# Sixty unread products of ones in the tail of a fused cross-attention, differential attention and expert-mixture kernel

## The reference, cut to what matters

```
x = x + cross_attention(ctx_1024, layernorm(x))      # 16 batches, 64 queries, 1601 + 64 keys, 16 heads of 64
x = x + differential_attention(layernorm(x))         # 16 heads, pairs of 8 columns, causal, group norm, Wo
x = x + experts(layernorm(x))                        # 8 experts, gates are a softmax over the two largest logits
# experts:
logits = x @ gate_w.T + gate_b ; keep the top 2, softmax
expert_out = einsum('bsd,edo->bseo', x, expert_w) + expert_b
out = einsum('bseo,bse->bso', expert_out, gate_score)
```

## Time and profile before

| what | us |
|---|---|
| median of 3 runs | 997.82 |
| lowest and highest of them | 996.78, 1000.93 |
| time of the profiled execution | 998.82 |
| its span | 997.1 |
| of that, what lies around the span | 1.72 |
| TensorE busy | 944.7 |
| mean granted clock of TensorE | 0.974 of full speed |

### The profile page before, as it was taken

How to read it: one execution, slowest core, us unless ns; L and a number is a source line. 1 busy time by engine, 2 the same in 40 slices (tenths; PEclk the granted TensorE clock), 3 DMA queues, 4 the chain that set the end, 5 groups by cost and what they waited for, 6 DMA issues and landing times.

```text
span 997.1 us, 19671 instructions
## 1 busy us (share of the span) xinstructions
PE 944.7 (95%) x7942; PEld 501.6 (50%) x7942; DVE 782.8 (79%) x1540; ACT 738.6 (74%) x1017; POOL 376.0 (38%) x376
## 2 busy tenths in 40 slices
PE   8679999999999999999999999999999998969975
PEld 5434455454545454545454545454545454547742
DVE  5968796969696969696969696969695956658965
ACT  4576878787878787878787878787878776635631
POOL 6471143433333343434343434343434223143343
PEclk9799999999999999999999999999999999979987
DMA  6212020302020312121212121121212000000000
GB/s 204 68 22 58 11 79 15 76 17 74 18 73 18 73 17 73 23 68 25 66 24 67 23 68 33 59 37 54 32 48 35 22 2 22 1 23 23 2 7 16
DMA packets 73218, 41.79 MB, mean 42 GB/s; under 512 B 60932, under 2 KB 68520, under 8 KB 73128
## 3 DMA queue, kind: packets, MB, share of 16 engines
q1 hardware_dynamic: 72840, 39.49, 16.4%
q10 hardware_dynamic: 288, 1.05, 0.3%
HBM read 25.98 MB, written 0.59 MB: 27 GB/s over the span
## 4 chain that ended last, share of the span: by engine, by line
PE 81%; DVE 13%; ACT 2%; issue 2%; POOL 1%; DMA 1%; POOLq 0%; ACTq 0%; DVEq 0%
PE S L1977 10%; PE S L1985 9%; PE S L1979 9%; PE OA L2006 9%; PE OA L2008 9%; PE OA L2010 9%; PE WW L1942 8%; PE WW L1958 1%; PE WW L1960 1%; DVE mx L1417 1%; PE WW L1959 1%; PE WW L1929 1%; DVE amx L720 1%; PE WW L1931 1%; PE WW L1930 1%
## 5 line engine op out<-in xcount | busy, mean ns | idle before, releaser
L1429 DVE TENSOR_TENSOR region<-S,region 128x1024 f16<-128x1024 f32 (+1 forms) x224 | 272.1, 1215 | 107.5 <-ACT S L1726 106.8
L1721 ACT ACTIVATE region<-S,sigma 128x1024 f16<-128x1024 f32 (+1 forms) x224 | 250.3, 1117 | 121.4 <-PE S L1985 121.4
L1417 DVE TENSOR_REDUCE mx<-WW 128x1 f32<-128x512 f32 (+1 forms) x480 | 263.6, 585 | 29.9 <-PE WW L1942 21.2
L1726 ACT ACTIVATE S<-S,sigma 128x1024 f32<-128x1024 f32 (+1 forms) x224 | 244.1, 1090 | 0.0
L1977 PE MATMUL S<-region,xT_hi 128*128 128x512 f16 (+1 forms) x416 | 124.3, 380 | 3.4 <-DVE region L1429 2.2
L2006 PE MATMUL OA<-region,xk 128*128 128x512 f16 (+1 forms) x416 | 124.4, 381 | 0.0
L1985 PE MATMUL S<-region,xT_lo 128*128 128x512 f16 (+1 forms) x416 | 124.2, 380 | 0.0
L2008 PE MATMUL OA<-region,xk 128*128 128x512 f16 (+1 forms) x416 | 124.2, 380 | 0.0
L1979 PE MATMUL S<-region,xT_hi 128*128 128x512 f16 (+1 forms) x416 | 124.1, 380 | 0.0
L2010 PE MATMUL OA<-region,xk 128*128 128x512 f16 (+1 forms) x416 | 124.0, 380 | 0.0
L1942 PE MATMUL WW<-xT_hi,region 128*128 128x512 f16 x360 | 120.3, 380 | 1.6 <-DVE region L1408 0.9
(11 more groups left out here) (296 smaller groups left out, 1728.3 us busy)
## 6 DMA issues: line engine op xcount, KB each, us to landing
raw<-ctx SPq DMA_DIRECT2D x16, 768.0 KB
rb<-inv_dram SPq DMA_DIRECT2D x16, 512.0 KB, 3.6
raw<-ctx SPq DMA_DIRECT2D x16, 32.5 KB
WO_lo<-L_xattn_Wq ACTq DMA_DIRECT2D x1, 512.0 KB, 3.9
WO_hi<-L_xattn_Wkv ACTq DMA_DIRECT2D x1, 512.0 KB, 4.8
lx<-x SPq DMA_DIRECT2D x1, 512.0 KB, 5.9
region<-L_xattn_Wo SPq DMA_DIRECT2D x1, 512.0 KB, 8.0
WO_hi<-L_xattn_Wkv SPq DMA_DIRECT2D x1, 512.0 KB, 8.9
```

Source lines behind the costliest of these rows:

```text
L1417: nc.vector.tensor_reduce(mx[:, r, c:c + 1], W[BANK[("m", n)]][:, 0:width], AX.X, ALU.max)\
L1429: nc.vector.tensor_tensor(p_lo[k][0:r, :], src, p_hi[k][0:r, :], ALU.subtract)\
L1721: nc.scalar.activation(p_hi[k][0:r, :], src, ACT.Exp, scale=sigma[0:r, 0:1])
L1726: nc.scalar.activation(src, src, ACT.Exp, scale=sigma[0:r, 0:1]).then_inc(e_done.sem, 1)
```

## The change

A helper issues a number of float32 products of `ones` by `ones` (128x128 by 128x128) into columns 384 to 511 of the first bank of `OA`. Nothing reads them. 24 of them stand at the head of `side_transposes(1)`, 6 at the head of `side_transposes(7)`, 6 at the head of `side_transposes(8)` and 18 between `side_products(9)` and `expert_bias(2)`. No wait, copy or transfer is added, and nothing else moves.

```
+            def idle_products(count):
+                for _ in range(count):
+                    mm(OA[:, 0, 384:512], ones[:], ones[:], start=True, stop=True)
+
             def side_transposes(n):
 
+                idle_products({1: 24, TB - 1: 6, TB: 6}.get(n, 0))
                 if n <= TB:
                     wait(pe, "oc", Turn(n - 1))
                     for c in range(2):
...
             experts(2)
             side_transposes(SIDES)
             side_products(SIDES)
+            idle_products(18)
             expert_bias(2)
             experts(3)
             expert_bias(3)
```

## The result

| | before | changed |
|---|---|---|
| median of 11 runs, us | 996.78 | 1002.72 |
| lowest and highest | 993.31, 1001.21 | 1000.43, 1008.98 |
| ratio, with 95% interval | | 1.0064 (1.0037 to 1.0091) |
| time and span of the profiled execution | 998.82, 997.1 | 1000.43, 998.7 |

A forecast was written before the change was run, and what follows sets the result against it. It took the last 115 us to count, engines handing on one chain with little slack. 998.82 - 0.2 + 1.27 - 0.9 + 4.03 = 1003.0 us, the profiled execution being 1.0 us above the median: 1002.0 us, range 998.5 to 1005.8.

The forecast's parts named there:

- within 0.5%: Measured time within 0.5%, 5.0 us, of no change: chance 0.63, against 0.33 for slower and 0.04 for faster.
- Price of a product: Each added float32 product is two records of 0.112 us, 0.224 us at full clock and 0.426 us at half.
- Place A: 24 products ahead of side 1, inside a 6.01 us TensorE stand: -0.2 us, bounds 0 and -1.4.
- The half microsecond of room: Ahead of side 1, 5.4 us of products were to end near 887.6 us, half a microsecond inside the stand.
- Place B: 6 products ahead of side 7, where TensorE has no stand: +1.27 us, bounds 0.5 and 2.6.
- Place C: 6 products ahead of side 8, inside a 2.05 us stand: half clock later and shorter, -0.9 us, bounds 0 and -2.0.
- Place D: 18 products ahead of the bias of tile 2, no stand, VectorE waiting: +4.03 us, bounds 3.7 and 7.7.
- rival 1: Half clock, its fall put off at C, covers the 18 products: +3.6 us, 1005.6 us; chance 0.15.
- The last stand: 5.16 us TensorE stand ahead of the bias of tile 4: stays as long, half clock mostly stays behind it, 0 us.
- Rivals 2, 3 and 4: 2: clock holds at A and C, 999.7 us, chance 0.15; 3: also in the last stand, 997.3 us, 0.05.
- rival 4: Products far cheaper than projections' records, or VectorE not waiting for tile 3's experts: about 998 us; chance 0.05.

The follow-up runs named there:

- A alone: Kernel before with only the 24 products ahead of side 1: 997.57 us against 997.80, ratio 0.9996.
- B alone: Kernel before with only the 6 products ahead of side 7: 1000.59 us, ratio 1.0027.
- D alone: Kernel before with only the 18 products ahead of the bias of tile 2: 1004.84 us, ratio 1.0066.

## Why the prediction was right, point by point

The direction and the main mechanism held, and the measured 1002.72 us lies in the range. 4.2 us were forecast, 5.9 were measured between medians, and the chances leaned to "within 0.5%" where 0.64% was measured. Part of this agreement is luck. On the terms of the profiled executions, from the heads of side 1 on, the cost was 7.2 us; 998.82 + 7.2 = 1006.0 us, a little above the range. The interval of the medians, 3.7 to 9.1 us, tells neither 4.2 nor 7.2 from what was measured. Places C and D each came out 1.6 to 1.7 us dearer than forecast.

- **Price of a product.** Held. 36 records in 4.19 us at full clock, 0.116 us each for the 0.112 taken. The 56 ns that the prediction estimated from the page TensorE: Matmul & The Clock Gate of the Trainium skill, section "Back-to-back issue gap", do not hold for these float32 products: 0.23 us. That section calls its formula the gap of an isolated matmul and gives some 81 ns at 128 columns for a stream with weight loads, which the prediction left out; that is too low for these as well.
- **Place A, -0.2 us.** Held: -0.06 in the profile, ratio 0.9996 alone. The half microsecond of room was not there: the products took 5.62 us, not 5.4, ended as the source did, and overran it in the execution with A alone. In the profiles of the seven kernels without these products the stand measures 4.95 to 6.01 us, and the prediction read it where it was longest. The next stand grows from 2.18 to 3.74 us, and the clock falls. The prediction had 3.4 us for it; with a copy that keeps its distance of 5.63 us and 1.56 us saved before it, it had to be 3.7. That the low clock behind this second stand is what keeps the gain away is shown by filling it too: 8.18 us.
- **Place B, +1.27 us.** Held: VectorE's wait of 1.26 us, 1.35 us on the stretch. B alone moved the median by 2.8 us, with a clock that was low for longer. No run filled the place with a larger or smaller number.
- **Place C, -0.9 us.** This is one of the two terms that were off. It measured +0.8 us in the changed kernel, 0.5 from the biases to the gate products and 0.3 in these, and -0.6 us alone, with a ratio of 1.0004: nothing that the medians show, within some 2.5 us. Where the clock falls, ahead of the biases or behind them, the low stretch covers most of the experts of tile 2 either way. Filling the stand of 1.9 us ahead of the biases was what it took.
- **Place D, +4.03 us.** The path was right: one step later the same products cost nothing. The size was off, 5.59 us in the changed kernel and 6.02 alone, because the low stretch reached into them. That was rival 1, given 0.15 and 3.6 us. It came in part, 1.6 us. The forecast had treated it as a case beside the others, where it belonged into the term as an average: in the changed kernel C's late fall and D's higher price are the same low stretch. The reason that rival 1 gives, the fall put off at C, is not needed for it: D alone has no products at C and shows 6.02 us.
- **The last stand, 0.** Held for the changed kernel: 5.16 us, and half clock behind it, of which the experts of tiles 5 and 6 caught a little less (5.57 us for 6.08).
- **Rivals 2, 3 and 4** did not come. The clock did not hold at A, at C or in the last stand of the changed kernel (5.16 us, low at its end). It held at A and C only where the neighbouring stand was filled too, and in the last stand where 22 products stood in it or 18 just ahead of its last part. With every stand filled, and without B and D, the kernel is 7 to 9 us faster than before. Against rival 4 stand the 0.23 us a product and VectorE's wait of 12.57 us.

## What to carry to other kernels

Work that only keeps TensorE's clock up is free where TensorE stands, and has its full price a few instructions away, where another engine is waiting for what stands behind it. Look for the stand in the timeline before placing it, and ask which stand comes next: filling one of two neighbouring stands gained 0.1 to 0.5 us on the stretch and nothing in the median, filling both gained 1.6 us on the stretch. Leave some room in a stand, too: its length in one profile is not its length in every execution. Unread work ahead of a product that another engine has been waiting for is the worst place, the more so while the clock is low.

## What was not expected

Products of 4.1 us in front of the experts of tile 4 left a stand of 1.15 us and brought the experts of tiles 5 and 6 from 6.08 to 3.70 us, without delaying anything: a hidden delay of a product that nobody is waiting for did as well as filling the stand (ratio 0.9966 and 0.9958). And half clock can outlast dense work: with B alone it held for 17 us, from 965.4 to 982.4 us, in which TensorE was busy 15.24 us, from 972.8 to 981.7 us without a stand:

```profile
965.40:982.40 17.00, 15.24 (x26) 6.82 (x26) 6.41 (x29) 3.88 (x16) 5.81 (x8) 0.50 0.03 8
```

The scatter of one kernel between executions, some 8 us, goes with this clock. Of the 29 runs of the kernel before that stand beside the single places, the five with a mean granted clock of 0.977 took 994.1 to 997.0 us, the six with 0.969 to 0.971 took 999.1 to 1002.9 us. Part of it arises in the main part, whose program the change leaves alone. The heads of side 1 stand anywhere from 882.4 to 888.4 us in the twelve profiles. They stand at 882.4 to 883.2 us in the three without half clock between 60 and 875 us, the changed kernel's among them, at 884.0 and 884.4 us in two with one short low stretch near 71 us, and at 886.5 to 888.4 us in the seven with more, that of the kernel before among them. At one such place TensorE's rows are, before,

```profile
836.36 1.75 PE L560 MATMUL WW<-ident,raw 128*128 128x128 f32 x7 [3.32 <-DVE raw L579]
```

and changed, at full clock:

```profile
832.56 0.98 PE L560 MATMUL WW<-ident,raw 128*128 128x128 f32 x7 [1.27 <-DVE raw L579]
```

Near 68 us the stand is even the same, 2.15 us in both, and from 71 to 75 us the clock is 0.57 in one and 1.00 in the other. What decides whether the clock falls in such a place is not shown. So two profiles of this kernel are compared from one fixed instruction to the next, and a gain of clock in one profile is not yet a gain of the kernel.
